# Gated expert layer on one core: routing weights of 12 of 16 expert groups are spread by transfers, silu is written in place, three small stages change queue positions

## The reference, cut to what matters

```
x = x + wkv(w, u, k=layernorm(x), v=ctx)      # (16, 64, 256), a scan over 64 positions
x = x + moe(layernorm(x))                     # 1024 tokens, 32 experts, 8 chosen per token

# moe, for h = layernorm(x), 1024 tokens x 256:
probs = softmax(h @ gate_w)                   # 1024 x 32
w, sel = top_k(probs, 8); w = w / sum(w)      # every expert takes at most 512 tokens, in token order
for each expert e:
    g = h @ w_gate[e]; u = h @ w_up[e]        # 256 x 96 each
    out += w[:, e] * (silu(g) * u) @ w_down[e]   # 96 x 256
```

## Time and profile before

| | us |
|---|---|
| median of 3 runs (267.11 to 268.24) | 267.29 |
| the profiled execution, its own time | 268.78 |
| its span, first to last instruction | 267.0 |
| PE busy | 243.3 |
| DVE / ACT / POOL busy | 136.0 / 132.7 / 151.2 |

### The profile page before, as it was taken

How to read it: one execution, slowest core, us unless ns; L and a number is a source line. 1 busy time by engine, 2 the same in 40 slices (tenths; PEclk the granted TensorE clock), 3 DMA queues, 4 the chain that set the end, 5 groups by cost and what they waited for, 6 DMA issues and landing times.

```text
span 267.0 us, 4296 instructions
## 1 busy us (share of the span) xinstructions
PE 243.3 (91%) x1403; PEld 203.1 (76%) x1406; DVE 136.0 (51%) x349; ACT 132.7 (50%) x242; POOL 151.2 (57%) x140
## 2 busy tenths in 40 slices
PE   6567799999899979999999699999999999999994
PEld 2324689897688768788888578888888888888883
DVE  4598765683469626773885426242423333233333
ACT  2885658434883567258653712234444352535320
POOL 5128651358956783669574302349585867677630
PEclk9858999999999997999999979999999999999999
DMA  6940661000505242060504100000505050710002
GB/s 203 268 128 16 170 175 32 2 1 4 165 12 130 69 109 69 4 184 12 156 23 130 47 1 2 0 0 2 147 32 157 24 160 20 213 42 0 2 0 79
DMA packets 38413, 19.96 MB, mean 75 GB/s; under 512 B 29944, under 2 KB 38392, under 8 KB 38392
## 3 DMA queue, kind: packets, MB, share of 16 engines
q1 hardware_dynamic: 37544, 19.27, 25.0%
q10 hardware_dynamic: 848, 0.43, 0.5%
HBM read 18.65 MB, written 1.05 MB: 74 GB/s over the span
## 4 chain that ended last, share of the span: by engine, by line
PE 72%; DVE 11%; issue 7%; ACT 3%; DMA 3%; POOL 2%; ACTq 1%; DVEq 0%; POOLq 0%
PE bank L735 44%; PE bank L756 22%; DMA ctx_sb<-in_ctx_dram 3%; PE bank L693 2%; DVE t_sb L1118 1%; PE bank L742 1%; DVE t_sb L1112 1%; DVE bank L978 1%; ACT s_sb L585 1%; DVE mixed L1017 1%; POOL t_lo L417 1%; ACT t_hi L592 1%; POOL wlo L388 1%; DVE inv L989 1%; POOL rstd L396 1%
## 5 line engine op out<-in xcount | busy, mean ns | idle before, releaser
L417 POOL TENSOR_TENSOR t_lo<-t_sb,t_hi 128x512 fp32r<-128x512 f32 (+1 forms) x53 | 61.9, 1167 | 86.1 <-ACT t_hi L592 84.4
L735 PE MATMUL bank<-h_hi,whi 128*128 128x512 f32 (+1 forms) x216 | 85.6, 396 | 3.9 <-issue 3.2
L388 POOL TENSOR_TENSOR wlo<-raw,whi 128x768 fp32r<-128x768 f32 x42 | 77.3, 1843 | 13.6 <-ACT whi L555 13.3
L735 PE MATMUL bank<-h_hi,wlo 128*128 128x512 f32 (+1 forms) x216 | 80.7, 374 | 0.0
L735 PE MATMUL bank<-h_lo,whi 128*128 128x512 f32 (+1 forms) x216 | 80.4, 372 | 0.0
L592 ACT ACTIVATE t_hi<-t_sb 128x512 fp32r<-128x512 f32 (+1 forms) x54 | 31.5, 584 | 94.8 <-DVE t_sb L1118 94.5
L1112 DVE TENSOR_TENSOR t_sb<-bank,s_sb 128x512 f32<-128x512 f32 (+1 forms) x54 | 34.0, 630 | 78.8 <-PE bank L742 40.7
L756 PE MATMUL bank<-whi,t_hi 128*128 128x256 f32 x192 | 50.3, 293 | 0.7 <-ACT t_hi L592 0.7
L735 PEld LDWEIGHTS bank<-h_hi,whi 128*128 128x128 f32 x216 | 41.5, 192 | 10.0 <-issue 4.0
L756 PE MATMUL bank<-wlo,t_hi 128*128 128x256 f32 x192 | 48.6, 284 | 0.0
L735 PEld LDWEIGHTS bank<-h_hi,wlo 128*128 128x128 f32 x216 | 41.1, 190 | 7.9
(11 more groups left out here) (111 smaller groups left out, 189.7 us busy)
## 6 DMA issues: line engine op xcount, KB each, us to landing
raw<-in_L_ffn_w_gate_dram SPq DMA_DIRECT2D x14, 384.0 KB
raw<-in_L_ffn_w_up_dram SPq DMA_DIRECT2D x14, 384.0 KB
raw<-in_L_ffn_w_down_dram SPq DMA_DIRECT2D x42, 128.0 KB
out_dram<-x SPq DMA_DIRECT2D x4, 256.0 KB, 2.5
x_sb<-in_x_dram SPq DMA_DIRECT2D x1, 512.0 KB, 7.0
ctx_tile<-in_ctx_dram SPq DMA_DIRECT2D x4, 128.0 KB, 5.8
x_sb<-in_x_dram SPq DMA_DIRECT2D x1, 256.0 KB, 3.3
ctx_sb<-in_ctx_dram SPq DMA_DIRECT2D x1, 256.0 KB, 3.8
```

Of the source, the lines that this page charges most:

```text
L388: pool.tensor_tensor(split_view(wlo, slot, part), raw_parts(slot, part), split_view(whi, slot, part).bitcast(F32), ALU.subtract).then_inc( ...
L417: pool.tensor_tensor(t_lo[k % 2][:, c], t_sb[:, c], t_hi[k % 2][:, c].bitcast(F32), ALU.subtract).then_inc(t_lo_ready, 1)
L735: last = nc.tensor.matmul(ps[:, c], up_weight(w, slot, part, k, j), h[:, k, tokens], start=(i == 0), stop=(i == len(terms) - 1))
```

## The change

1. In the turns `it` = 1 to 3 of both halves the matmul at L742 goes: 12 of 18. The other six, four of 256 columns in turn 0 of the first half and two of 512 in turn 0 of the second, stay. Instead PE makes, once per half, the 32 rows of routing weights in float32 (`turn_rows`, one matmul of 32 x 512 into bank 7), ACT copies them to `rows` (`keep_rows`), and a transfer from ACT's own queue spreads four rows over 128 partitions (`spread_rows`, 256 KB each) into one of four buffers `w_sb`.
2. In the same turns silu is written in place, into g's PSUM bank. ACT then doesn't wait for the t1 before it, but PE's u of step n now waits for t1 of step n-1 (`t1_ready`), where it waited for silu of step n-1.
3. `keep_low` goes ahead of `product_low` in POOL's step at `at` = 2.
4. `logits` goes from the end of PE's step at `at` = 1 to `at` = 2, between u and g. `largest` on DVE goes from `at` = 1 to `at` = 2, and `exps` of the next unit goes ahead of `route_exps` on ACT.
5. `turn_parts` goes from the end of PE's step at `at` = 4 to the middle of the next one, between g and the down product (not for the last unit).
6. ACT's and DVE's loops over the turns 1 and 2 of the second half are written out.

The diff, cut to its core:

```diff
@@ -125,6 +125,10 @@
+        rows = sb("rows", [E, T])
+        SPREAD = 4
+        w_sb = [sb(f"w_sb{i}", [P, HALF]) for i in range(SPREAD)]
@@ -165,6 +169,7 @@
+        rows_ps = bank[7][0:E, :]
@@ -227,6 +232,8 @@
+        rows_ready, rows_kept = sem("rows_ready"), sem("rows_kept")
+        w_landed = [sem(f"w_landed{i}") for i in range(SPREAD)]
@@ -256,7 +263,6 @@
-        FIRST_SPREADS = GROUPS + 2
@@ -265,10 +271,11 @@
-        def spreads_before(half, it):
-            if half:
-                return it * 2 + FIRST_SPREADS
-            return it * 2 + 2 if it else 0
+        def spread_of(half, position):
...
+            n = half * (GROUPS - 2) + position - 2
+            return n % SPREAD, n // SPREAD + 1
@@ -419,12 +426,14 @@
+                        if tiles:
+                            tiles[0](it, k)
...
-                            tiles(it, k)
+                            tiles[1](it, k)
@@ -438,11 +447,14 @@
-                elif at == 2:
...
+            def tiles_before(it, k):
+                at, back, _, _ = cycle(it, k)
+                if at == 2:
...
-                turn(0, it, WHOLE, tiles=tiles_beside, split=(1, 2) if it < TURNS - 1 else (1,))
+                turn(0, it, WHOLE, tiles=(tiles_before, tiles_beside), split=(1, 2) if it < TURNS - 1 else (1,))
@@ -577,12 +589,32 @@
-            def step(n, k, p, between=(), tiles=None):
+            def keep_rows(half):
...
+                act.wait_ge(rows_ready, half + 1)
+                nc.scalar.activation(rows[:, half * HALF:(half + 1) * HALF], rows_ps, ACT.Copy).then_inc(rows_kept, 1)
...
+            def spread_rows(half, position):
...
+                act.wait_ge(rows_kept, half + 1)
+                buffer, use = spread_of(half, position)
+                if use > 1:
...
+                    n = half * (GROUPS - 2) + position - 2 - SPREAD
+                    before, at = divmod(n, GROUPS - 2)
+                    act.wait_ge(t1_ready, steps_before(before, 0) + (TURN_STEPS if not before else 0) + (at + 2) * GT + GT + 1)
+                first = first_group(half, position // 2) + position % 2
+                row = rows[first * EG:(first + 1) * EG, None, half * HALF:(half + 1) * HALF]
+                act.dma_start(w_sb[buffer][:], row.to_broadcast([EG, QI, HALF])).then_inc(w_landed[buffer], 16)
...
+            def step(n, k, p, between=(), tiles=None, in_place=False):
...
                 act.wait_ge(g_ready, n + 1)
-                act.wait_ge(t1_ready, n + 1)
-                nc.scalar.activation(s_sb[:, c], g_ps(k)[:, c], ACT.Silu).then_inc(s_ready, 1)
+                if not in_place:
+                    act.wait_ge(t1_ready, n + 1)
+                to = g_ps(k) if in_place else s_sb
+                nc.scalar.activation(to[:, c], g_ps(k)[:, c], ACT.Silu).then_inc(s_ready, 1)
                 for stage in between:
@@ -594,7 +626,7 @@
-                        step(steps_before(half, it) + (p or 0) * TURN_STEPS + k, k, p, beside.get((p or 0, k), []), tiles and (lambda: tiles(it, k)))
+                        step(steps_before(half, it) + (p or 0) * TURN_STEPS + k, k, p, beside.get((p or 0, k), []), tiles and (lambda: tiles(it, k)), in_place=it > 0)
@@ -604,9 +636,13 @@
-                                (0, 5): [lambda: take_route(second_routed)]}, split=(2,))
+                                (0, 5): [lambda: take_route(second_routed)],
+                                (1, 1): [lambda: keep_rows(0), lambda: spread_rows(0, 2)],
+                                (1, 3): [lambda: spread_rows(0, 3)]}, split=(2,))
...
+                if (it, k) in ((1, 0), (1, 1), (1, 3), (2, 0)):
+                    spread_rows(0, {(1, 0): 4, (1, 1): 5, (1, 3): 6, (2, 0): 7}[it, k])
@@ -615,16 +651,20 @@
-                    route_exps(routed)
...
+                    route_exps(routed)
...
-            turn(1, 0, WHOLE, {(0, 0): [lambda: take_route(later_routed(LATER[-1]))]}, split=(2,))
-            with act.Fori(1, TURNS - 1) as it:
-                turn(1, it, WHOLE)
+            turn(1, 0, WHOLE, {(0, 0): [lambda: take_route(later_routed(LATER[-1]))],
+                               (0, 1): [lambda: keep_rows(1), lambda: spread_rows(1, 2)],
+                               (0, 2): [lambda: spread_rows(1, 3)],
+                               (0, 3): [lambda: spread_rows(1, 4)],
+                               (0, 4): [lambda: spread_rows(1, 5)]}, split=(2,))
+            turn(1, 1, WHOLE, {(0, 3): [lambda: spread_rows(1, 6)]})
+            turn(1, 2, WHOLE, {(0, 0): [lambda: spread_rows(1, 7)]})
@@ -716,14 +756,17 @@
-            def project(n, half, p, part, slot, j, group):
+            def project(n, half, p, part, slot, j, group, in_place=False):
...
+                elif part == 1 and in_place:
+                    pe.wait_ge(t1_ready, n + 1)
@@ -741,6 +784,13 @@
+            def turn_rows(half):
...
+                if half == 0:
+                    pe.wait_ge(counted, 1)
+                nc.tensor.matmul(rows_ps, expert3[:], route[:, half * HALF:(half + 1) * HALF], start=True, stop=True).then_inc(rows_ready, 1)
@@ -785,13 +835,16 @@
-                            project(n, half, p, 1, slot, j, group + slot)
+                            project(n, half, p, 1, slot, j, group + slot,
+                                    in_place=it > 1 or it == 1 and k > 0 or half == 1 and first_turn and k == 0)
+                        if tiles:
+                            tiles[0](it, k)
...
-                        if j == 0:
+                        if j == 0 and first_turn:
@@ -809,7 +862,7 @@
-                            tiles[0](it, k)
+                            tiles[1](it, k)
@@ -825,7 +878,7 @@
-                            tiles[1](it, k)
+                            tiles[2](it, k)
@@ -850,29 +903,35 @@
                                 (1, 0): [first_counts],
+                                (1, 1): [lambda: turn_rows(0)],
                                 (1, 5): [lambda: turn_mixed(third)]},
                  {(0, 2): [lambda: turn_h(second)]})
+            def tiles_within(it, k):
+                at, _, routed, _ = cycle(it, k)
+                if at == 2:
+                    logits(routed)
...
             def tiles_beside(it, k):
                 at, back, routed, front = cycle(it, k)
-                if at == 1:
+                if at == 0 and back.n > LATER[0]:
+                    turn_parts(later_routed(back.n - 1))
+                elif at == 1:
                     turn_h(back)
...
             def tiles_after(it, k):
-                at, back, routed, front = cycle(it, k)
-                if at == 1:
-                    if front:
-                        turn_kv(front)
-                    logits(routed)
-                elif at == (4 if front else 2):
-                    if front:
-                        turn_mixed(front)
+                at, _, routed, front = cycle(it, k)
+                if at == 1 and front:
+                    turn_kv(front)
+                elif at == 4:
+                    turn_mixed(front)
+                elif at == 2 and not front:
                     turn_parts(routed)
...
             for it in range(1, TURNS):
-                turn(0, it, WHOLE, tiles=(tiles_beside, tiles_after))
-            turn(1, 0, WHOLE)
+                turn(0, it, WHOLE, tiles=(tiles_within, tiles_beside, tiles_after))
+            turn(1, 0, WHOLE, {(0, 0): [lambda: turn_rows(1)]})
             for it in range(1, TURNS - 1):
@@ -1103,13 +1162,19 @@
-            def step(n, k, p, spreads):
+            def step(n, k, p, half, it):
...
-                dve.wait_ge(w_turned, spreads)
+                if it == 0:
+                    dve.wait_ge(w_turned, (4 if half else (p or 0) * 2) + k // GT + 1)
+                    w, gate = w_ps, s_sb
+                else:
+                    buffer, use = spread_of(half, it * 2 + k // GT)
+                    dve.wait_ge(w_landed[buffer], use * 16)
+                    w, gate = w_sb[buffer], g_ps(k)
...
-                nc.vector.tensor_tensor(t1_sb[:, c], w_ps[:, c], s_sb[:, c], ALU.mult).then_inc(t1_ready, 1)
+                nc.vector.tensor_tensor(t1_sb[:, c], w[:, c], gate[:, c], ALU.mult).then_inc(t1_ready, 1)
@@ -1158,8 +1222,8 @@
+                elif at == 2:
...
-                elif at == 2:
@@ -1174,7 +1238,7 @@
-            with dve.Fori(1, TURNS - 1) as it:
+            for it in range(1, TURNS - 1):
```

More of the change, by code:

```diff
@@ L1122, in turn @@
                     for k in range(TURN_STEPS):
-                        step(steps_before(half, it) + (p or 0) * TURN_STEPS + k, k, p,
-                             spreads_before(half, it) + (p or 0) * 2 + k // GT + 1)
+                        step(steps_before(half, it) + (p or 0) * TURN_STEPS + k, k, p, half, it)
                         for stage, u in beside.get((p or 0, k), []):
```

## The result

The changed kernel takes **287.65 us** (median of 4 runs, 287.12 to 288.0) against 267.2 (266.94 to 268.24): a ratio of 1.0756, 95% interval 1.0721 to 1.0791. It is slower by 20 us; 256.3 had been forecast.

The account below looks back on a forecast made before the run. PE was taken to bound the kernel, busy 243.3 of 267.0 us, with waits for late routing stages in the first half. Spreads -2.0, keep_low -4.15, logits -3.94, `turn_parts` -0.95 sum to -11.0: 256.3 us, range 254.4 to 260.6.

Parts of the forecast that it names:

- Nothing from them.: The 256 KB transfers land well before their use, the first having about 10 us: cost 0.
- Rival (c): First transfer takes 13.2 us on four engines, making step 12's t1 up to 3 late: 259.3 us; chance 0.06.
- The signs: Wrong if PE waits for t1 at u, first-half clock falls under 0.9 after 63 us, or half isn't about 9 shorter.
- Rival (d): Each issue on ACT's queue holds ACT longer: 259.2 us at 3.24, 274 at 4.5; chance 0.04 past turning point 3.9.
- Moves: keep_low, logits (with largest and exps) and `turn_parts` moved: -4.15, -3.94 and -0.95 us, together -9.0.
- keep_low: End of first half: 3.23 us wait before g and 1.82 slow stretch go, 0.9 rest stays: net -4.15.
- (b): The 3.23 us wait at the first half's end isn't the copy's and stays with its slow stretch: 260.4; chance 0.08.
- Spreads: Twelve PE spreads go (-2.76), two row matmuls come (+0.46), 0.3 for ACT's lateness: -2.0 us.
- Logits and `turn_parts`: First half: logits' waits of 0.95 and 1.82 and a 1.57 slow stretch go, 0.4 stays: -3.94; `turn_parts` waits go: -0.95.
- Rests: PE waits left in the first half: 0.4 us at logits, 0.5 at ranks, 0.4 at `turn_parts`.
- (a): Lowered clock returns after the rests at logits or the first half's end: 258 us, both 259.7; chance 0.20.
- Silu in place, cost 0: Silu takes 0.58 us either way; PE's new wait for t1 has time to spare: cost 0, bounds 0 and 2.

Follow-up runs that it names:

- sixteen rows: Changed kernel with each row of routing weights kept four times, so each transfer has sixteen source rows, same bytes: 256.53 us, ratio 0.9551; again 256.34 us.
- dead transfers: Kernel before, plus the same twelve four-row transfers from a constant tile into buffers that nothing of the computation reads: 295.59 us, ratio 1.10.

## Why the prediction was wrong

**The step that failed** is one sentence on the transfers: "Nothing from them." I had asked whether they land in time for the t1 that reads them, and they do, but for one wait of 2.3 us. I had not asked what they sit in front of. Measured, the term is +31.1 us: 287.65 less the 256.5 of sixteen rows. In the two traces, with spans of 286.3 and 255.0: 17.56 and 8.79 of waits, and behind them (4.75 - 2.79) + (4.50 - 2.79) = 3.67 of slow matmuls, 30.0 of the 31.3. The path is shown: four engines (132 packets), loads that stand unfinished at 2 tenths of DMA, SP's three issues of 22.41 us, `whi`, silu, t1, PE. What makes the issue itself wait on SP is not shown; that the transfers bring it about is, by the runs without them and with sixteen rows.

**Rival (c)** had the rule and about the duration (four times 3.3, 13.2 us; it is 10.5), but priced it at the t1 alone, "The wait would stand at that t1 alone". It should have been multiplied: twelve transfers x 13.2 = 158 us on each of four engines. Those engines also carry a quarter of w_gate's and w_up's packets and all of w_down's, some 7.5 us for each of 14 groups in the view of before, 105 us as an estimate; together 263, in a kernel of 267. Five transfers were issued from 53.4 to 77.9 us, around the load issued at 66.7. A chance of 0.04 for slower was too low beside that sum. Measured over the whole kernel, the transfers' packets took 91 us of each of the four engines, (8.4% x 286.3 - 0.5% x 267.0) x 16 / 4, less than twelve times 10.5: beside the loads a packet took 0.18 us on average (19.3% x 16 x 29 / 506), and alone 0.31. Why, no run shows.

**The signs** that the prediction named for itself were met: transfers that take 10.5 us and not under 10, a t1 that waits for a DMA, a stretch of the first half with a clock well under 0.9 (0.55 from 104.2 to 109.6 us), and a PE that waits for t1 at a u, 8.79 us. This last one is not the doing of silu in place: the version with dead transfers, which has the waits of before, waits 8.67 at the same matmul, for silu.

**Rival (d)**, the slower one, named the wrong queue. It feared that an issue on ACT holds ACT; those took 0.54, and 1.14 for the longest. It was SP's issue that was held, by what ACT had sent.

**The other steps held in the main.** In the version with sixteen rows, where the failed term is taken away, the forecast 256.3 met 256.5 and 256.3. Moves: -9.6 for -9.0. keep_low: -4.4 for -4.15, and the copy was the releaser, as named, so (b) falls. Spreads: -2.8, or 256.4 - 258.88 = -2.5 by difference, for -2.0. Logits and `turn_parts` were measured only together with keep_low; the difference is -5.2 for -4.89. Rests: 0.44, 0.55, 0.20 for 0.4, 0.5, 0.4. (a) did not come: at both places the clock stays at 1.00 with these rests. Still, the kernel before and the one with keep_low alone show that after waits of the same length the clock may fall or not, so a priced slow stretch is a chance and not a fixed term, and that the 1.57 in the logits term came out may be in part luck. The chances of the forecast and of (a) to (c) add up to 0.95, where 0.94 is given for faster.

**Silu in place, cost 0**: right, but for half of the reason. It costs nothing, and it is also what keeps one input of t1 in PSUM, once the weights have left it. As an option to be left out, it is worth 7.3 us.

The best version is the one with sixteen source rows: 4.3% faster than the kernel before (4.5% in the first set of runs), 11% faster than the changed one.

## What to carry to other kernels

When transfers move to another queue, ask how many engines each uses, multiply its time by their number, and lay that beside the loads that share those engines: a load is done only when its slowest engine is. Look for loads that already sit on few engines, as w_down's do here; whether spreading those helps is not tested. Copying a source row a few times, so that eight or sixteen rows stand outermost, took away the 31 us. And when an operand leaves PSUM, look at the other operand and at what POOL reads at the time.

## What the runs showed of the hardware that I had not expected

- Transfers from four source partitions moved 25 GB/s in all, and a 2 KB packet took 0.31 us of its engine, but 0.18 us on average beside the weight loads. Where each transfer had a single source partition and sat on all engines, it took 0.98 us, so that sixteen engines moved 29 GB/s.
- Loads whose source has four experts outermost ran on about a quarter of the DMA engines (24.9%, 87 GB/s), and w_gate's and w_up's on all.
- A DMA issue on SP was held for 17.04 us, for most of which the DMA engines were busy at 2 tenths.
- DVE's product of two SBUF tiles took 0.68 to 2.31 us beside POOL, and always 0.69 with one of them in PSUM; POOL's own went from 1.84 to 2.05.
- After PE's wait of 1.8 us at the same place, the granted clock of the next 4.5 us was 1.00 in one kernel, and 0.63 in the window of before.
